# Fewer early key loads at the end of a projection stage, its weight conversions moved up, and its value copies moved to VectorE

## The chip, the cores and the metric

The kernel runs on one core of a Trainium2 chip. The metric is the device time in microseconds (us) of one execution; several executions are timed and their median counts. The engines are TensorE (PE, matrix products), VectorE (DVE), ScalarE (ACT), GpSimd (POOL) and SyncE (SP), which here issues every transfer on one queue of the core's 16 DMA engines.

## What is computed

A transformer layer over 4096 rows of 512 numbers: causal attention with 16 heads of 32, then a gated feed-forward net whose weights come as integers. In short:

```python
q, k, v = split(x @ Wqkv, 3)
q, k = layernorm(q) * q_ln_scale, layernorm(k) * k_ln_scale
attn = softmax(causal(q k^T / sqrt(32)))          # per head
x = layernorm(x + (attn @ v) @ out_W)
Wg, Wu, Wd = ((w - 128) * scale for w in (gate_w, up_w, down_w))
x = layernorm(x + (silu(x @ Wg^T) * (x @ Wu^T)) @ Wd^T)
```

## The kernel before

Three stages follow one another, each a block of its own with one program for each engine: `project` (to about 331 us), `attend` (to about 1540 us) and `finish`. What one stage hands to the next lies in DRAM or in buffers that all stages know (`keep`).

**The projection** walks over 8 chunks of 512 rows. A chunk has 12 units, one for each of its 4 row tiles and each of queries, keys and values (`m` = 0, 1, 2): PE multiplies a tile of rows with 512 columns of the weights, each number split into a high and a low part, so 12 products (L403) into one of four `acc` banks. For queries and keys DVE measures and normalises the rows (`measure`, `apply`); for values ACT copies the bank to `v_out` (`take_v`, L500 to 503) and SP stores it. The normalised rows of a chunk are then turned in 8 jobs (4 of queries, 4 of keys). For a job PE turns four 128x128 pieces (L425), ACT makes squares and the high half of the scaled result (`high`, L491 to 498), DVE the low half (`low`, L575), and SP stores both halves (L321). The halves lie in one of four part buffers, and ACT writes a buffer only once its former stores have landed (`parts_stored`).

The jobs of a chunk run beside the units of the next one. In the last chunk `plan` takes another order of the units (`final`): first the 8 units of queries and keys, beside which the jobs of the chunk before run, in units 1 to 7, and then the 4 units of values, 8 to 11, beside which the chunk's own 8 jobs run, two in each.

Beside all that the integer weights of the last stage are turned to float, 6 blocks of 256 KB a chunk: SP loads a block (L290), ACT turns it (`turn_float`, L510), DVE finds its largest number (`widest`, L601), SP stores it (L294). There are two buffers, so block e + 2 is loaded once block e is turned. Before the change block e is turned in unit 2e.

At the end of the projection DVE works out two flags from the largest norms and weights; the engines read them when the attention begins.

**Loads of the attention.** The attention takes its 4 groups of 4 heads one after the other, and in each group the 8 chunks of queries; chunk c meets c + 1 blocks of keys. A key load (`key_load`, L73 to 78) is three transfers of 256 KB, each to 32 partitions (high, low and high again), and for the first group one of 16 KB (`one_load`); a query load is three such transfers and one of 16 KB; a load of values is one of 256 KB. Each chunk's first score waits for its queries and its own key block. In the last chunk of the projection SP already issues loads for the first group, in `ahead(j)`, L333 to 349: with j = 0 keys 0, queries 0 and values 0, and with j = 1 and 2 keys 1 and 2. When the attention begins, SP issues, in this order, queries 1, [keys and] values 1, queries 2, [keys and] values 2, keys and values 3 to 7, stores of the context, and queries 3; keys below `AHEAD` are left out there.

Of the kernel before, what the change touches and what calls it, by code (L numbers as in the profile page):

```python
# [30 lines left out]
F32 = mybir.dt.float32  # L31
# [16 lines left out]
ST = CH // P  # L48
DC = D // P
# [7 lines left out]
BOUND = 60.0  # L57
WHOLE = 4096.0
ROWS = 3 * HD + 2
AHEAD = 3  # L60


def over_chunks(engine, body):
# [42 lines left out]
BLOCKS = 3 * IC // ST  # L106
# [21 lines left out]

def weight_load(sp, dr, keep, to, j):

    sp.dma_start(to.bitcast(F32), dr["wq"].rearrange("(b t) p d -> b p t d", t=ST)[j]).then_inc(keep["w_in"][j], 16)


def store_chunk(sp, dr, keep, g, ch):
# [26 lines left out]
def project(nc, io, dr, keep):  # L161


    ACCS = 4
    NU, NJ = 3 * ST, 2 * DC
# [4 lines left out]


    x_parts = {0: (0,), 1: (1, 2), 2: (3,)}

    def plan(before, after):

# [10 lines left out]
    with ExitStack() as c:  # L186
# [18 lines left out]
        v_out = sb("v_out", [P, 2, D])  # L205
# [25 lines left out]
        x_in = [sem(f"x_in{dc}") for dc in range(DC)]  # L231
        x_high = sem("x_high")
        x_low = sem("x_low")
        wqkv_in = [[sem(f"wqkv_in{dc}{m}") for m in range(3)] for dc in range(DC)]
        w_high_done = sem("w_high_done")
        w_low_done = sem("w_low_done")
        ident_ready = sem("ident_ready")
# [30 lines left out]
        @block.sync  # L268
        def _(sp):
            def load_x(n, dc):  # L270
                sp.dma_start(x_raw[:, dc, :], xs[dc][:, bass.ds(n * CH, CH)]).then_inc(x_in[dc], 16)

            for dc in range(DC):
                load_x(0, dc)
                for m in range(3):
                    cols = slice(m * D, (m + 1) * D)
                    sp.dma_start(w_raw[:, dc, cols], io["wqkv"][dc * P:(dc + 1) * P, cols]).then_inc(wqkv_in[dc][m], 16)
            sp.dma_start(scales[:, 0, :], io["q_scale"]).then_inc(scales_in, 16)
            sp.dma_start(scales[:, 1, :], io["k_scale"]).then_inc(scales_in, 16)
            sp.wait_ge(dconst, 1)  # L280
            for u in range(4):
                sp.dma_start(dr["shift"].rearrange("a h (p u s) -> u (a h p) s", u=4, p=4)[u], zeros[:]).then_inc(zero_stored, 16)
            sp.dma_start(dr["one_rows"].rearrange("a (h s) -> (a h) s", h=HG), one_fill[:]).then_inc(zero_stored, 16)
            sp.dma_start(ow_raw[:], io["out_w"].rearrange("(g r) e -> r g e", r=P)).then_inc(ow_in, 16)
            for s_, k in ((parts_stored, 32), (v_stored, 16), (wq_stored, 16)):
                for one in s_:
                    sp.sem_inc(one, k)

            def load_int(n, e):
                sp.dma_start(wq_int[:, e % 2, :], io["wq"][bass.ds(n * WT + e, 1)].rearrange("a p x -> (a p) x"))\  # L290
                  .then_inc(int_in[e % 2], 16)

            def store_float(n, e):
                sp.dma_start(dr["wq"][bass.ds(n * WT + e, 1)].rearrange("a p x -> (a p) x"), wq_f[:, e % 2, :])\  # L294
                  .then_inc(wq_stored[e % 2], 16)

            load_int(0, 0)
            load_int(0, 1)

            def body(n, c, par, before, after, half):  # L300
                for dc in range(DC if after else 0):

                    sp.wait_ge(x_low, DC * n + dc + 1)
                    sp.nop(nofuse=True)
                    load_x(n + 1, dc)
                for u, ((st, m), jobs) in enumerate(plan(before, after)):
                    if m == 2:
                        sp.wait_ge(v_taken, ST * n + st + 1)
                        sp.nop(nofuse=True)
                        sp.dma_start(dr["v"].rearrange("(t p) d -> t p d", p=P)[bass.ds(n * ST + st, 1)].rearrange("t p d -> (t p) d"),  # L310
                                     v_out[:, st % 2, :]).then_inc(v_stored[st % 2], 16)
                    for own, i in jobs:

                        o = n if own else c
                        sp.wait_ge(high_done, NJ * o + i + 1 + 2)
                        sp.nop(nofuse=True)
                        sp.wait_ge(low_done, NJ * o + i + 1 + 2)
                        sp.nop(nofuse=True)
                        g = i % DC
                        for part, to in ((part_hi, ("q_hi", "k_hi")), (part_lo, ("q_lo", "k_lo"))):  # L320
                            sp.dma_start(dr[to[i // DC]][g * P:(g + 1) * P, bass.ds(o * CH, CH)], part[:, i % 4, :].bitcast(F32))\  # L321
                               .then_inc(parts_stored[i % 4], 16)
                    if u % 2 == 0:
                        e = u // 2
                        sp.wait_ge(floated, WT * n + e + 1)
                        sp.nop(nofuse=True)
                        store_float(n, e)
                        if after or e + 2 < WT:
                            load_int(n, e + 2)
                    if not after and u in (1, 3, 5):  # L330
                        ahead(u // 2)

            def ahead(j):  # L333

                if j == 0:
                    sp.wait_ge(w_low_done, 3 * DC)
                    sp.nop(nofuse=True)
                    sp.wait_ge(zero_stored, 80)
                    sp.nop(nofuse=True)
                    for one in parts_stored:  # L340
                        sp.wait_ge(one, 32 + 64 * AHEAD)
                        sp.nop(nofuse=True)
                    for one in v_stored:
                        sp.wait_ge(one, 16 + 32)
                        sp.nop(nofuse=True)
                    sp.wait_ge(fin_pool, 1 + NG)
                    sp.nop(nofuse=True)
                key_load(sp, dr, keep, 0, j, keep["k_in"][j])
                one_load(sp, dr, keep, j, keep["k_in"][j])
                if j == 0:  # L350
                    query_load(sp, dr, keep, 0, 0, 0, keep["q_in"][0])
                    value_load(sp, dr, keep["first_values"][:], 0, 0, keep["v_in"][0])

            over_chunks(sp, body)
# [121 lines left out]
        def _(act):  # L476
# [35 lines left out]
            def body(n, c, par, before, after, half):  # L512
                for u, ((st, m), jobs) in enumerate(plan(before, after)):
                    if not before and u == 4:
                        act.wait_ge(ow_in, 16)
                        act.activation(ow_hi[:], ow_raw[:], ACT.Copy).then_inc(ow_high, 1)
                    if m == 1 and after and st in x_parts:

                        if before and st == 0:
                            act.wait_ge(acc_full, NU * n)  # L520
                        for dc in x_parts[st]:
                            high_x(n + 1, 1 - par, dc)
                    if m == 2:
                        take_v(n, u, st)
                    for own, i in jobs:
                        high(n if own else c, i)
                    if u % 2 == 0:
                        turn_float(n, u // 2)

            over_chunks(act, body)  # L530

# [1 line left out]
        def _(dve):  # L533
# [54 lines left out]
            def apply(n, par, u, st, i):  # L588
                dve.wait_ge(rstd_ready, 2 * ST * n + 2 * st + i + 1)
                dve.tensor_scalar(normed[:, par, i, st, :], acc[u % ACCS][:], mv[:, i, 0:1], rstd[:, i:i + 1],  # L590
                                  ALU.subtract, ALU.mult).then_inc(qk_normed, 1)

            def top(o, i):

                dve.wait_ge(norms_done, NJ * o + DC * (i + 1) + 2)
                dve.tensor_reduce(norm_max[:, i, bass.ds(o, 1)], norms[i][:], AX.X, ALU.max).then_inc(norms_read, 1)
# [6 lines left out]
            def body(n, c, par, before, after, half):  # L603
# [3 lines left out]
                for u, ((st, m), jobs) in enumerate(steps):  # L607
# [8 lines left out]
                    for t in tops:  # L616
                        if t[2] <= u:
                            top(*t[:2])
                    tops = [t for t in tops if t[2] > u]
                    for own, i in jobs:  # L620
                        low(n if own else c, i)
                        if i % DC == DC - 1:
                            tops.append((n if own else c, i // DC, u + 3))
                    if u % 2:
                        widest(n, u // 2)
                for t in tops:
                    top(*t[:2])

# [496 lines left out]
def finish(nc, io, dr, keep):  # L1125
# [7 lines left out]
    with ExitStack() as c:  # L1133
# [23 lines left out]
        slot = [[c.enter_context(nc.psum_tensor(f"slot{s}{b}", [P, CH], F32)) for b in range(2)] for s in range(2)]  # L1157
        y = [c.enter_context(nc.psum_tensor(f"y{st}", [P, D], F32)) for st in range(ST)]

        w_in, small_in = keep["w_in"], keep["small_in"]  # L1160
        ident_zero = sem("ident_zero")
        ident_ready = sem("ident_ready3")
        half_ready = sem("half_ready")
# [123 lines left out]
        def _(pe):  # L1287
# [50 lines left out]
            def program(v):  # L1338

                def gate_up(j, pos, n, par, i, first_chunk):  # L1340
# [3 lines left out]
                        pe.wait_ge(slot_free, t_end(n) + FREE)  # L1344
                    if first_chunk:
                        for j in range(3 * i // ST, (3 * i + 2) // ST + 1):
                            pe.wait_ge(w_in[j], 16)
                    for q in range(2):
                        w = tile(i, q)
                        for dc in range(DC):  # L1350
# [202 lines left out]
def build(nc, io):  # L1553
# [14 lines left out]
    with ExitStack() as c:  # L1568
# [9 lines left out]
            "q_in": [sem(f"q_in{b}") for b in range(3)],  # L1578
            "wq_stored": [sem(f"wq_stored{b}") for b in range(2)],
            "gate_scale": sb("gate_scale_sb", [P, IC], F32), "up_scale": sb("up_scale_sb", [P, IC], F32),  # L1580
            "small_in": sem("small_in"), "w_in": [sem(f"w_in{j}") for j in range(BLOCKS)],
            "ctx_in": [sem(f"ctx_in{h}") for h in range(HALF)], "x_res_in": [sem(f"x_res_in{h}") for h in range(HALF)],
            "inv_ready": sem("inv_ready"), "c_scaled": sem("c_scaled"), "c_high": sem("c_high"), "c_ready": sem("c_ready"),
            "ctx_taken": sem("ctx_taken"), "sums_taken": sem("sums_taken"),
# [53 lines left out]
```

## Time and profile before

| | us |
|---|---|
| runs of the kernel, median (lowest to highest) | 2370.82 (2368.36 to 2372.7) |
| the profiled execution | 2370.67 |
| its span, from first to last instruction | 2368.9 |

In that span PE is busy for 2308.9 us, DVE for 1775.2, ACT for 1291.7 and POOL for 245.3; the mean clock granted to TensorE is 0.988 of full speed. A row of a timeline gives the start and the duration in us, the engine, the line of the kernel, the operation, the tile that is written and those that are read, the shapes, how many instructions were merged, and in brackets how long the engine had been idle before and what ended that.

### The profile page before, as it was taken

Reading aid. Unit: us, or ns where it says so; the run is one execution under the profiler, and the core shown is the slowest. Engines: PE = TensorE matmul, PEld = TensorE weight load, DVE = VectorE, ACT = ScalarE, POOL = GpSimd, SP = SyncE. Lnnn points to the kernel's source line nnn. Section 1 sums busy time; section 2 is a strip of 40 time slices with the busy share of each in tenths; the row PEclk is TensorE's granted clock in tenths of the full one; section 3 lists DMA queues with packets and bytes.
Section 4 is the critical chain, followed back from the end, with each engine's and each line's share of the span. In section 5 each row is a group of like instructions: output and inputs, shape, how many; then the busy total and the mean of one; then the engine's idle time right before and its main releaser. Section 6 shows DMA issues by size and latency. Waiting matters only on the chain. (4 is left out here: it accounts for less than half of the span.)

```text
span 2368.9 us, 34364 instructions
## 1 busy us (share of the span) xinstructions
PE 2308.9 (97%) x12556; PEld 1424.3 (60%) x12578; DVE 1775.2 (75%) x1821; ACT 1291.7 (55%) x1631; POOL 245.3 (10%) x269
## 2 busy tenths in 40 slices
PE   8999979999999999999999999989999999999997
PEld 7888844444444444444444444378888888888885
DVE  7777748998889988899898998945556556465554
ACT  4444458888888888888888888711111111111111
POOL 2111112110021100211002110000000000000000
PEclk9999979999999999999999999989999999999998
DMA  7767785100821008210082101441111021110100
GB/s 252 254 238 252 231 255 106 33 23 6 179 56 33 24 6 170 60 33 24 6 165 64 33 24 41 147 151 36 36 36 54 22 69 36 37 54 18 36 19 18
DMA packets 126303, 197.50 MB, mean 83 GB/s; under 512 B 14489, under 2 KB 39577, under 8 KB 126113
## 3 DMA queue, kind: packets, MB, share of 16 engines
q1 hardware_dynamic: 126128, 195.25, 29.4%
q8 instruction: 101, 1.65, 0.3%
q14 instruction: 74, 0.60, 0.1%
HBM read 122.83 MB, written 72.37 MB: 82 GB/s over the span
## 5 line engine op out<-in xcount | busy, mean ns | idle before, releaser
L1041 ACT ACTIVATE probs<-score 128x1024 f32<-128x1024 f32 (+3 forms) x1152 | 1000.2, 970 | 176.1 <-PE score L953 174.6
L1104 DVE TENSOR_TENSOR total<-total,probs 128x2048 f32<-128x2048 f32 (+3 forms) x468 | 983.2, 2101 | 79.3 <-POOL probs L915 22.1
L953 PE MATMUL score<-queries,keys 98*128 98x512 f32 (+3 forms) x2304 | 641.7, 406 | 12.1 <-ACTq L1025 6.2
L953 PEld LDWEIGHTS score<-queries,keys 98*128 98x128 f32 x2304 | 380.9, 189 | 434.2 <-ACT probs L1041 350.3
L1416 ACT ACTIVATE hidden<-slot,gate_scale_sb 128x512 f32<-128x512 f32 x128 | 88.2, 689 | 633.8 <-PE slot L1352 633.8
L969 PE MATMUL ctx_acc<-probs,values 128*32 128x512 f32 (+3 forms) x3584 | 421.6, 561 | 0.0
L1478 DVE SCALAR_TENSOR_TENSOR hidden<-slot,up_scale_sb,hidden 128x512 f32<-128x512 f32 x128 | 96.0, 750 | 252.9 <-ACT hidden L1416 252.9
L915 POOL TENSOR_SCALAR_AFFINE_SELECT probs<-probs 128x512 f32<-128x512 f32 x128 | 167.3, 1308 | 1010.3 <-ACT probs L1041 1010.3
L1352 PE MATMUL slot<-xt_hi,w_front 128*128 128x512 f32 x608 | 238.5, 392 | 1.5 <-DVE xt_lo L1519 1.5
L1352 PE MATMUL slot<-xt_lo,w_front 128*128 128x512 f32 x608 | 238.1, 392 | 0.0
L969 PEld LDWEIGHTS ctx_acc<-probs,values 128*32 128x32 f32 x3584 | 85.5, 109 | 193.6 <-issue 148.6
L403 PE MATMUL acc<-w_hi,x_hi 128*128 128x512 f32 x384 | 164.2, 428 | 7.4 <-DVE w_lo L558 7.4
L1352 PE MATMUL slot<-xt_hi,w_back 128*128 128x512 f32 x416 | 163.4, 393 | 0.0
L1352 PE MATMUL slot<-xt_lo,w_back 128*128 128x512 f32 x416 | 162.1, 390 | 0.0
L403 PE MATMUL acc<-w_hi,x_lo 128*128 128x512 f32 x384 | 151.5, 394 | 0.0
L403 PE MATMUL acc<-w_lo,x_hi 128*128 128x512 f32 x384 | 151.0, 393 | 0.0
L969 PE MATMUL ctx_acc<-probs,first_values 128*32 128x512 f32 (+3 forms) x1024 | 132.8, 591 | 0.7 <-ACT ctx_out L1030 0.7
L1352 PEld LDWEIGHTS slot<-xt_hi,w_front 128*128 128x128 f32 x608 | 115.1, 189 | 26.2 <-DVE xt_lo L1519 1.7
L1352 PEld LDWEIGHTS slot<-xt_lo,w_front 128*128 128x128 f32 x608 | 115.0, 189 | 23.9
L1270 POOL TENSOR_TENSOR rstd<-veps,minus_half 128x1 f32<-128x1 f32 x64 | 36.2, 566 | 792.2 <-DVE veps L1442 792.2
L1363 PE MATMUL y<-w_front,h_hi 128*128 128x512 f32 x288 | 112.1, 389 | 0.0
L1363 PE MATMUL y<-w_front,h_lo 128*128 128x512 f32 x288 | 112.1, 389 | 0.0
(121 smaller groups left out, 2199.6 us busy)
## 6 DMA issues: line engine op xcount, KB each, us to landing
keys<-k_hi SPq DMA_DIRECT2D x64, 256.0 KB
queries<-q_hi SPq DMA_DIRECT2D x64, 256.0 KB
wq_int<-in_wq SPq DMA_DIRECT2D x48, 256.0 KB, 3.2
wq_float<-wq_f SPq DMA_DIRECT2D x48, 256.0 KB, 2.8
x_raw<-in_x_t SPq DMA_DIRECT2D x32, 256.0 KB, 3.7
v_rows<-v_out SPq DMA_DIRECT2D x32, 256.0 KB, 2.5
q_hi<-part_hi SPq DMA_DIRECT2D x32, 256.0 KB, 2.6
q_lo<-part_lo SPq DMA_DIRECT2D x32, 256.0 KB, 2.8
```

The source lines that it names most:

```text
L403: ins = pe.matmul(bank[:], x[:, par, dc, rows], w[:, dc, m * D:(m + 1) * D], start=dc == 0 and a == 0, stop=dc == DC - 1 and a == 2)
L915: pool.affine_select(out=view, in_=view, compare_op=ALU.is_ge, fill=0.0, base=0, pattern=[[0, HG], [1, P]], channel_multiplier=-1).then_in ...
L953: ins = pe.matmul(score[u % RING][:, i, cut(t):], keys[0:ROWS, kb // ST, h, kb % ST * P:(kb % ST + 1) * P], queries[0:ROWS, q_buffer[ch], ...
L969: ins = pe.matmul(ctx[h * HD:(h + 1) * HD, n0:], value(kb)[:, h * HD:(h + 1) * HD], probs[:, t % PB, h, n0:], start=t in first, stop=t in ...
L1041: act.activation(probs[:, t % PB, 2 * p:2 * p + 2, cut(t):], score[u % RING][:, :, cut(t):], ACT.Exp).then_inc(exped, 1)
L1104: dve.tensor_tensor(into, into, now, ALU.add).then_inc(added, 1)
L1270: pool.tensor_tensor(rstd[:, k, st:st + 1], veps[:, k, st:st + 1], minus_half[:], ALU.pow).then_inc(rooted[k], 1)
L1352: ins = pe.matmul(slot[pos % 2][q][:], v(w[:, dc * P:(dc + 1) * P]), v(x[:, par, dc, :]), start=dc == 0 and a == 0, stop=dc == DC - 1 and ...
L1363: ins = pe.matmul(y[st][:], v(x[:, st * P:(st + 1) * P]), v(tile(i, 2)), start=i == 0 and a == 0, stop=i == IC - 1 and a == 1)
L1416: act.activation(hidden[:, i % 2, :], slot[pos % 2][0][:], ACT.Silu, scale=gate_scale[:, i:i + 1]).then_inc(gated, 1)
L1478: dve.scalar_tensor_tensor(hid, slot[pos % 2][1][:], up_scale[:, i:i + 1], hid, ALU.mult, ALU.mult)\
```

## The change

- `AHEAD` is 1 in place of 3: of the loads for the attention only keys, queries and values 0 are issued in the projection, in unit 1 of the last chunk. Keys 1 and 2 are issued by SP in the attention, ahead of values 1 and 2.
- In the last chunk the six blocks of weights are turned in units 0, 1, 3, 4, 6 and 7 in place of 0, 2, 4, 6, 8 and 10. Their loads and stores on SP go with them, and DVE's reductions come one unit later each.
- In the last chunk DVE copies the values in place of ACT.
- The semaphores of the projection's weight loads are used again for the weight loads of the last stage, which now wait for 32 in place of 16.

```diff
-AHEAD = 3
+AHEAD = 1
...
-    sp.dma_start(to.bitcast(F32), dr["wq"].rearrange("(b t) p d -> b p t d", t=ST)[j]).then_inc(keep["w_in"][j], 16)
+    sp.dma_start(to.bitcast(F32), dr["wq"].rearrange("(b t) p d -> b p t d", t=ST)[j]).then_inc(keep["weights_in"][j], 16)
...
+    def float_units(after):
+
+        return [0, 2, 4, 6, 8, 10] if after else [0, 1, 3, 4, 6, 7]
...
-        wqkv_in = [[sem(f"wqkv_in{dc}{m}") for m in range(3)] for dc in range(DC)]
+        wqkv_in = [keep["weights_in"][3 * dc:3 * dc + 3] for dc in range(DC)]
...
-                    if u % 2 == 0:
-                        e = u // 2
+                    if u in float_units(after):
+                        e = float_units(after).index(u)
...
-                    if not after and u in (1, 3, 5):
-                        ahead(u // 2)
+                    if not after and u == 1:
+                        ahead(0)
...
-                    if m == 2:
+                    if m == 2 and after:
                         take_v(n, u, st)
...
-                    if u % 2 == 0:
-                        turn_float(n, u // 2)
+                    if u in float_units(after):
+                        turn_float(n, float_units(after).index(u))
...
+            def take_v(n, u, st):
+                dve.wait_ge(acc_full, NU * n + u + 1)
+                dve.wait_ge(v_stored[st % 2], 32 * n + 16 * (st // 2) + 16)
+                dve.tensor_copy(v_out[:, st % 2, :], acc[u % ACCS][:]).then_inc(v_taken, 1)
...
+                    if m == 2 and not after:
+                        take_v(n, u, st)
...
-                    if u % 2:
-                        widest(n, u // 2)
+                    if u - 1 in float_units(after):
+                        widest(n, float_units(after).index(u - 1))
...
-                            pe.wait_ge(w_in[j], 16)
+                            pe.wait_ge(w_in[j], 16 + 16)
```

## Rows read from the trace of the kernel before

**Rows 1.** Windows: start:end, length, busy us of each engine, granted clock, DMA share, GB/s
```profile
300.00:310.00 10.00, 7.02 (x37) 5.49 (x37) 4.30 (x7) 5.34 (x9) 0.54 (x1) 1.00 1.05 307
310.00:320.00 10.00, 6.75 (x30) 5.19 (x31) 3.41 (x5) 5.07 (x10) 0.00 (x0) 0.87 1.04 394
...
330.00:336.00 6.00, 0.08 (x1) 0.00 (x0) 0.80 (x4) 0.00 (x0) 0.00 (x0) 0.50 0.03 10
336.00:340.00 4.00, 3.71 (x10) 2.72 (x10) 0.00 (x0) 2.39 (x3) 0.32 (x1) 0.50 0.52 140
340.00:384.00 44.00, 44.00 (x278) 19.17 (x277) 34.72 (x22) 34.95 (x47) 15.74 (x12) 0.91 1.09 202
...
400.00:500.00 100.00, 99.82 (x632) 42.70 (x624) 93.14 (x46) 85.73 (x98) 11.39 (x9) 1.00 0.13 33
```

**Rows 2.** Timeline of ACT in the last chunk of the projection
```profile
296.59 0.69 ACT L497 ACTIVATE squares<-turn,mix_root 128x512 bf16<-128x512 f32 x1 [2.57 <-DMA q_lo<-part_lo]
297.18 0.68 ACT L498 ACTIVATE part_hi<-turn,scales 128x512 fp32r<-128x512 f32 x1
297.78 0.63 ACT L510 ACTIVATE wq_f<-wq_int 128x512 f32<-128x512 int32 x1
...
315.46 0.69 ACT L497 ACTIVATE squares<-turn,mix_root 128x512 bf16<-128x512 f32 x1 [1.25 <-issue]
...
322.76 0.60 ACT L503 ACTIVATE v_out<-acc 128x512 f32<-128x512 f32 x1 [1.74 <-PE acc L403]
```

**Rows 3.** Timeline of PE, the turns of the last chunk's own parts
```profile
303.48 0.63 PE L425 MATMUL turn<-ident,normed_qk 128*128 128x128 f32 x4 [1.25 <-DVE normed_qk L590]
...
307.59 0.60 PE L425 MATMUL turn<-ident,normed_qk 128*128 128x128 f32 x4
309.92 0.63 PE L425 MATMUL turn<-ident,normed_qk 128*128 128x128 f32 x4 [1.72 <-ACT part_hi L498]
...
317.61 1.09 PE L425 MATMUL turn<-ident,normed_qk 128*128 128x128 f32 x4 [1.67 <-ACT part_hi L498]
...
322.57 0.60 PE L425 MATMUL turn<-ident,normed_qk 128*128 128x128 f32 x4
```

**Rows 4.** Timeline of SP: the first issue of keys 1 and of keys 2
```profile
291.18 0.45 SPq L76 DMA_DIRECT2D keys<-k_hi  x1
...
296.40 0.60 SPq L76 DMA_DIRECT2D keys<-k_hi  x1
```

**Rows 5.** Timeline of PE in the attention: first scores, chunk 1's, chunk 3's
```profile
336.29 5.89 PE L953 MATMUL score<-queries,keys 98*128 98x512 f32 x16 [6.21 <-ACTq L1025]
...
343.98 2.08 PE L953 MATMUL score<-queries,keys 98*128 98x512 f32 x4
...
385.73 1.66 PE L953 MATMUL score<-queries,keys 98*128 98x512 f32 x6 [0.88 <-DMA queries<-shift]
```

**Rows 6.** Integer blocks, 289 to 303 us: durations min/median/max in ns, starts, landing
```profile
L290 SPq DMA_DIRECT2D wq_int<-in_wq x3: 552/670/929, 289.5 to 302.2; - x3
...
DMA to landing us min/median/max: 8.2/11.9/12.1
```

**Rows 7.** Timeline of DVE: last normalised rows, last reduction of a block, flags
```profile
302.54 0.80 DVE L590 TENSOR_SCALAR normed_qk<-acc,mv,rstd 128x512 f32<-128x512 f32 x1
...
326.62 0.67 DVE L601 TENSOR_REDUCE whole<-wq_f 128x1 f32<-128x512 f32 x1
...
330.75 0.16 DVE L641 CAST flags<-flag_f 1x2 int32<-1x2 f32 x1
```

**Rows 8.** Loads of values 2 and of values 7: issue and landing, columns as rows 6
```profile
L99 SPq DMA_DIRECT2D values<-v_rows x1: 400/400/400, 341.4 to 341.4; - x1
...
DMA to landing us min/median/max: 8.4/8.4/8.4
...
L99 SPq DMA_DIRECT2D values<-v_rows x1: 393/393/393, 366.4 to 366.4; - x1
...
DMA to landing us min/median/max: 15.1/15.1/15.1
```

More of the change, by code:

```diff
@@ L1158, in finish @@
         y = [c.enter_context(nc.psum_tensor(f"y{st}", [P, D], F32)) for st in range(ST)]
-        w_in, small_in = keep["w_in"], keep["small_in"]
+        w_in, small_in = keep["weights_in"], keep["small_in"]
         ident_zero = sem("ident_zero")
@@ L1580, in build @@
             "gate_scale": sb("gate_scale_sb", [P, IC], F32), "up_scale": sb("up_scale_sb", [P, IC], F32),
-            "small_in": sem("small_in"), "w_in": [sem(f"w_in{j}") for j in range(BLOCKS)],
+            "small_in": sem("small_in"), "weights_in": [sem(f"weights_in{j}") for j in range(BLOCKS)],
             "ctx_in": [sem(f"ctx_in{h}") for h in range(HALF)], "x_res_in": [sem(f"x_res_in{h}") for h in range(HALF)],
```

## The prediction

> **What bounds the kernel now.** I read the windows first, then the timelines of ScalarE (ACT), TensorE (PE), VectorE (DVE) and SyncE (SP) over the end of the projection, then the landings of single transfers, then PE at the start of the attention. In the attention PE is busy 99.8% of the time [rows 1], so whatever delays PE there is paid in full, and two places matter: the last chunk of the projection and the first 60 us behind it. In the last chunk the DMA engines are saturated: their share is 1.05 and 1.04 in 300 to 320 us [rows 1], while PE is busy 7.02 and 6.75 of each 10 us. The ACT rows show why. A part buffer (four of them) can be written again only when its stores have landed, and the squares wait for exactly that, 2.57 us for the low half of queries at 296.59 [rows 2]; where the row says "issue" (at 315.46) it is the same wait in the code. PE waits behind ACT: its turns stand idle 1.25, 1.72 and 1.67 us [rows 3], and at 317.61 four turns take 1.09 us in place of 0.63: after these gaps the granted clock fell to 1.2 GHz (mean 0.87 in 310 to 320 [rows 1]). The cause of the queue is in the SP rows: two further blocks of keys are fetched in the middle of it [rows 4]. Behind the projection the DMA engines idle, work at a share of 0.52 in 336 to 340, and then at 1.09 for the 44 us to 384 [rows 1]. That stretch ends on PE's path too: the first scores of chunk 3 wait 0.88 us for the last piece of its queries [rows 5].
>
> **Part 1: keys 1 and 2 leave the projection.** Two key loads are six transfers of 256 KB plus two of 16 KB, 1.61 MB. What it gives: without them the queue is gone by the time the last chunk's own eight parts run. Then PE goes from the first turn (303.48) to the seventh (322.57) [rows 3] without the waits. One pair of turns and one unit take 307.59 - 303.48 = 4.11 us, with no wait between them; there are three such periods, 12.3 us in place of 19.1 us. That is 6.8 us.
>
> **Part 2: floats two units earlier.** No instruction is added; six turnings, stores and integer loads keep their count. But ACT works in order, and turning block 4 now stands in unit 6, ahead of the squares of unit 7. Its integers are loaded in unit 3, at about 292 (where SP issued keys 1 at 291.18 [rows 4], and 0.9 us for the store and load that now stand ahead of chunk 0's loads). Integer loads took 8.2 to 12.1 us to land in this queue [rows 6]; the 8.2 belongs to the one that was not behind keys 1, so it lands at 300.2. From there: the turning to 300.9 (0.63), squares and high half to 302.2 (0.59 + 0.68) [rows 2], the low half to 302.9 (taken like the reduction, 0.7), the reduction to 303.5, the last normalised rows to 304.3 (0.80) [rows 7]. PE's first turn came right behind those rows (302.54 + 0.80, PE 303.48), so it moves to 304.4: a loss of 0.9 us. If the load takes 12.1 us the loss is 4.8 us; if it isn't late at all, zero.
>
> **Part 3: values by DVE.** Four copies leave ACT (0.60 us each [rows 2]) and go to DVE, where they cost about as much. DVE has room: it is busy 4.30 of 10 us and 3.41 of 10 us there [rows 1]. On the path the last copy holds ACT to 323.36 while the seventh turn has ended at 323.17: 0.2 us. The last reduction of a float block (326.62, 0.67 us, of which 0.6 before the next) leaves the end of DVE's chain to the flags: 0.6 us. If DVE's cover were gone the copies would cost 4 x 0.6 = 2.4 us.
>
> **The sum for the projection** is 6.8 - 0.9 + 0.2 + 0.6 = 6.7 us, between 2.8 (late integers) and 7.6. The flags, written at 330.75 [rows 7], come at about 324, and SP, PE and ACT start the attention as much earlier; the gap of 5 us behind the flags, with a DMA share of 0.03 [rows 1], stays. Shared semaphores and waits on 32 cost nothing: the weight loads of the last stage are counted from what the projection left, with no new producer.
>
> **Part 4: what comes back.** SP issues keys 1 now between queries 1 and values 1, keys 2 behind queries 2, and everything up to the queries of chunk 3 is queued behind them. Chunk 1's first score ran at 343.98 without a wait [rows 5]. It will wait for keys 1: at most 1.61 / 2 MB at 202 GB/s, 4.0 us, at least nothing; I take 2.5 us. This is not paid twice, since PE later waits again. At chunk 3 the queue decides: PE is there at 384.85 (385.73 - 0.88), its queries land at 385.73, and 1.61 MB more stand ahead of them. At the 202 GB/s of 340 to 384 [rows 1] this is 8.0 us. By landings it is more: values 2, issued at 341.4, landed 8.4 us later; values 7, issued at 366.4, 15.1 us later [rows 8]; 31.7 us for five pairs of keys and values, 6.3 us a pair, less 1.3 us for the 256 KB of values at 202 GB/s, 5.0 us a key load, 10.1 us for two. The lower end is the 394 GB/s of the stores in 310 to 320 [rows 1], 4.1 us. I take 9.0, between the two values of the stretch itself.
>
> In 340 to 384 the engines are as full (1.09) as in 310 to 320 (1.04) and move half as much. The Trainium skill has a rule for this (SBUF — State Buffer, Door 1: The DMA port swizzle): a transfer to 32 partitions reaches 8 of the 16 ports, and partitions 0 to 63 no more, so it gets half the bandwidth, 218 GB/s at most. Each piece of a key or query load goes to 32 partitions; by that figure the two loads would cost an estimated 7.4 us in the attention, and the trace's 202 GB/s agrees. The rule speaks against the change: loads of this kind are moved from beside stores, which use all partitions, to a stretch of loads of their own kind.
>
> **The clock.** PE stands still at chunk 3 from about 387.4 to 394.7 (in times of the kernel before), far longer than the gaps after which the clock fell at 317. It would restart at 1.2 GHz. At the start of the attention PE resumed at 336.29 and the clock came back at about 347.9 (0.91 mean over 44 us: 7.9 us of it at half), 11.6 us later [rows 1, 5]; six full scores took 1.66 us at full clock, four 2.08 us at half [rows 5], so PE loses about 0.45 us a microsecond: between 0 and 5.2 us. I take half, 2.6 us.
>
> **Sum.** -6.7 + 9.0 + 2.6 = +4.9 us. The profiled execution took 2370.67 us (span 2368.9 and 1.8 around it), the median of the runs is 2370.82: both are the same to 0.01%. 2370.67 + 4.9 = 2375.6 us.
>
> **Rivals.** (a) The stall at chunk 3 leaves the clock alone: +2.3 us, 2373.0. For it: gaps up to 1.72 us left it alone. Against: this gap is four times that. (b) Not slower: the two loads run in the attention at the stores' rate, 4.1 us, because SP issues keys 1 in 336 to 340, where the share is 0.52. Then -6.7 + 4.1 = -2.6, 2368.1. It decides at 6.7 us for the two, 240 GB/s; for over 0.2% faster they would have to cost under 2 us. Against: keys 1 are issued behind queries 1, and from 340 the engines are full. (c) The integers of block 4 are late as in the kernel before (12.1 us): the projection gives 2.8 in place of 6.7, in all +8.8, 2379.5. For it: the queue of chunk 0's loads stands ahead of them still. Against: keys 1 no longer do.
>
> **How the numbers follow.** A measurement of this kernel tells 0.2% (4.7 us) from no change, so "same" is 2366.1 to 2375.5. The forecast has 0.50, with its own range 2372 to 2380; (a) 0.18, (b) 0.14, (c) 0.18. Slower by over 0.2%: half of the forecast, nearly all of (c), little of (a): 0.45. Faster: under half of (b) and a remainder, 0.08. Same: 0.47. The range is 2367.5 (most of (b)) to 2381.
>
> **What would show it.** Squares in units 8 to 11 without waits for landings; the flags near 324; a wait of PE for keys 1 of about 2.5 us, then one of 5 to 8 us for the queries of chunk 3, and a granted clock of 0.5 behind it; windows near 100% after. The forecast is wrong if the wait at chunk 3 is under 3 us, or if the flags come later than 327.

## The result, and the profile after

| | before | after |
|---|---|---|
| median, us (20 runs each, side by side) | 2371.38 | 2375.56 |
| lowest to highest, us | 2368.36 to 2376.03 | 2371.91 to 2378.26 |
| ratio to before, 95% interval | 1 | 1.0017 (1.0012 to 1.0023) |
| profiled execution, us (its span) | 2370.67 (2368.9) | 2375.79 (2374.0) |

The changed kernel is slower by 4.2 us of the medians; that is little, but the interval leaves 1 out. 2375.6 us was predicted.

First the windows, with the columns of [rows 1]:

```profile
300.00:310.00 10.00, 7.43 (x30) 5.75 (x30) 6.44 (x12) 4.84 (x8) 0.55 (x1) 0.83 0.99 376
310.00:320.00 10.00, 9.59 (x54) 7.86 (x54) 5.58 (x8) 5.74 (x10) 0.00 (x0) 1.00 0.72 273
...
340.00:384.00 44.00, 40.55 (x264) 17.41 (x264) 33.07 (x20) 33.05 (x42) 10.30 (x8) 0.93 1.09 204
384.00:396.00 12.00, 7.21 (x28) 3.58 (x32) 5.04 (x3) 5.23 (x6) 0.64 (x1) 0.72 0.28 65
400.00:500.00 100.00, 99.82 (x639) 42.56 (x642) 92.95 (x47) 85.11 (x101) 14.65 (x10) 1.00 0.13 33
```

The window from 384 us before the change, which [rows 1] leaves out:

```profile
384.00:396.00 12.00, 10.85 (x67) 4.53 (x63) 7.90 (x4) 9.59 (x13) 1.27 (x2) 1.00 0.07 21
```

In 310 to 320 us PE is busy 9.59 of 10 us (6.75 before) while the DMA share has gone from 1.04 to 0.72: the queue in this part of the projection is gone. But in 340 to 384 PE, which was busy all 44 us before, loses 3.45 us with the DMA engines as full as they were (1.09), and in 384 to 396 it works 7.21 of 12 us, where it was 10.85, at a mean granted clock of 0.72, where it was 1.00. From 400 us on the windows agree.

The timelines give the places. PE and DVE at the end of the projection, to be held against [rows 3] and [rows 7] (the second and third row are the first products of unit 9):

```profile
304.37 0.63 PE L429 MATMUL turn<-ident,normed_qk 128*128 128x128 f32 x4 [2.57 <-DVE normed_qk L594]
...
305.51 0.90 PE L407 MATMUL acc<-w_hi,x_hi 128*128 128x512 f32 x1
306.21 0.63 PE L407 MATMUL acc<-w_lo,x_hi 128*128 128x512 f32 x1
...
318.18 0.60 PE L429 MATMUL turn<-ident,normed_qk 128*128 128x128 f32 x4
...
325.78 0.16 DVE L652 CAST flags<-flag_f 1x2 int32<-1x2 f32 x1
```

First to seventh turn take 13.81 us instead of 19.09, and the flags come 4.97 us sooner, at 325.78. ACT shows what delays the first turn (compare [rows 2]):

```profile
297.97 0.69 ACT L501 ACTIVATE squares<-turn,mix_root 128x512 bf16<-128x512 f32 x1 [4.36 <-DMA q_lo<-part_lo]
...
300.34 0.63 ACT L514 ACTIVATE wq_f<-wq_int 128x512 f32<-128x512 int32 x1 [1.10 <-DMA wq_int<-in_wq]
300.87 0.67 ACT L501 ACTIVATE squares<-turn,mix_root 128x512 bf16<-128x512 f32 x1
...
302.94 0.63 ACT L514 ACTIVATE wq_f<-wq_int 128x512 f32<-128x512 int32 x1 [0.81 <-DMA wq_int<-in_wq]
```

The integers of two blocks arrive after ACT has come to them (1.10 and 0.81 us), and behind these no squares name a landing any more. Ahead of them the squares still wait for one, 4.36 us and to 297.97, where it was 2.57 us and to 296.59. Then SP's first issue of the attention and PE's scores, against [rows 5]:

```profile
330.96 2.53 SPq L89 DMA_DIRECT2D queries<-q_hi  x2
```
```profile
331.25 5.89 PE L964 MATMUL score<-queries,keys 98*128 98x512 f32 x16 [6.14 <-ACTq L1036]
...
343.03 2.05 PE L964 MATMUL score<-queries,keys 98*128 98x512 f32 x4 [4.03 <-issue]
...
388.79 3.78 PE L964 MATMUL score<-queries,keys 98*128 98x512 f32 x8 [5.21 <-DMA queries<-shift]
```

The attention starts 5.04 us sooner, chunk 1 only 0.95 us sooner, because PE now waits 4.03 us there; chunk 3 starts 3.06 us later than before, after a wait of 5.21 us, and its scores run at half clock (eight take 3.78 us where six took 1.66). Matched product by product with the kernel before, PE's delay grows from 3.06 us there to 5.05 us at 400 us: the half clock accounts for the rest of the 5.1 us of span.

### The profile page after: what moved, and what is told of

It reads as the page before. It is cut to its first block and busy times, and to the rows that moved or that the text cites. A ratio compares the mean times of both kernels' runs of the same rounds, so it can differ in the third digit from the quotient of the medians.

```text
span 2374.0 us, 34368 instructions
## 1 busy us (share of the span) xinstructions
PE 2311.5 (97%) x12556; PEld 1425.5 (60%) x12578; DVE 1778.2 (75%) x1825; ACT 1289.6 (54%) x1627; POOL 246.8 (10%) x269
```

## Experiments

Each ratio is to the kernel before, run beside it on the same chip; three kernels were run once and stand outside the table. "The distance" is the time from SP's first issue of queries 1 to the first score of chunk 3, wherever PE waited for that: it is what the queue of the attention costs, with the start of the attention taken out. It is 49.85 us before (335.88 to 385.73) and 57.83 us after (330.96 to 388.79).

Flags, distances and waits are those of one profiled execution each. With the code of the projection unchanged the flags came at 328.69 to 331.41 us in four kernels (before, before with queries 3 early, narrow, wide), and at 323.34 and 326.89 in the two with keys 1 in unit 9. So two kernels' flags that lie less than about 3.5 us apart are not told from each other by them.

| kernel | ratio (95%) | flags at | distance | wait at chunk 3 |
|---|---|---|---|---|
| before | 1 | 330.75 | 49.85 | 0.88 |
| changed | 1.0017 (1.0012 to 1.0023) | 325.78 | 57.83 | 5.21 |
| loads alone | 1.0007 (0.9997 to 1.0016) | 323.64 | 56.84 | 0.78 |
| units alone | 1.0002 (0.9992 to 1.0011) | 332.45 | 49.12 | 1.28 |
| changed, queries 3 early | 0.9994 (0.9985 to 1.0004) | 324.24 | | none |
| before, queries 3 early | 0.9990 (0.9981 to 0.9999) | 331.41 | | none |
| changed, keys behind the stores | 1.0004 (0.9995 to 1.0014) | 326.56 | 49.65 | 2.11 |
| keys 1 in unit 9 | 0.9995 (0.9986 to 1.0004) | 323.34 | 52.44 | 3.75 |
| keys 1 in unit 9, queries 3 early | 0.9976 (0.9967 to 0.9985) | 326.89 | | none |
| keys 1 and 2 in units 9 and 10, queries 3 early | 0.9976 (0.9967 to 0.9985) | 323.94 | | none |
| the same as keys 1 in unit 9, queries 3 early, with the units of the change | 0.9966 (0.9955 to 0.9977) | 324.99 | | none |

### Which half does what

**The loads alone.** Only keys 0 are loaded in the projection; the floats and the copies of values stay as before.

```diff
-AHEAD = 3
+AHEAD = 1
...
-                    if not after and u in (1, 3, 5):
-                        ahead(u // 2)
+                    if not after and u == 1:
+                        ahead(0)
```

> Only keys 1 and 2 leave the projection; the floats keep units 0, 2, 4, 6, 8, 10 and ACT keeps the copies of the values. Theory (the queue of transfers holds the last chunk's turns; the two key loads come back ahead of the queries of chunk 3): the flags come 4 to 6 us earlier than in the kernel before, the attention loses 8 us at chunk 3 and 2 us of clock behind it: 4 to 6 us slower than before, about as the changed kernel, and the moved floats and copies are worth less than 2 us either way. Rival (it is the moved floats and copies that shorten the projection): the flags come less than 2 us earlier and the time is 8 us or more above the kernel before.

Measured: 2373.28 us against 2371.01, 2.3 us of the medians, smaller than expected and not told from nothing by the interval. PE and DVE:

```profile
340.71 2.05 PE L953 MATMUL score<-queries,keys 98*128 98x512 f32 x4 [3.39 <-issue]
...
386.06 1.66 PE L953 MATMUL score<-queries,keys 98*128 98x512 f32 x6 [0.78 <-DMA queries<-shift]
```
```profile
323.64 0.16 DVE L641 CAST flags<-flag_f 1x2 int32<-1x2 f32 x1
```

The flags come 7.1 us sooner: the projection's gain comes from the loads. That it is more than with the whole change (4.97 us) lies inside the scatter named above; 1.57 of the 2.14 us is the clock, which fell at the first turn in the changed kernel's profiled execution and not here (first to seventh turn 13.81 and 12.24 us). The queries of chunk 3 land 56.84 us after the first issue, 7.0 us more than before. That PE waited only 0.78 us for them isn't a better queue: PE was late itself. Its clock stayed at half until 354.1 us, after the wait for chunk 1; matched with the kernel before, PE was 6.73 us early at its first scores and 0.45 us late at 359 us, so that this wait of 3.39 us cost 7.2.

**The units alone.** Floats in units 0, 1, 3, 4, 6, 7 and values by DVE, keys 1 and 2 in the projection as before.

```diff
-                    if u % 2 == 0:
+                    if u in float_units(after):
...
-                    if m == 2:
+                    if m == 2 and after:
                         take_v(n, u, st)
...
```

> Only the floats and the copies of the values are moved; keys 1 and 2 stay in units 3 and 5 of the last chunk. Theory: the attention is as in the kernel before (wait of 0.9 us at chunk 3, no fall of the clock there); the projection gains little, 0 to 2.5 us, because the queue stays: 0 to 2.5 us faster than before. Rival (floats and copies are the gain): the flags come 4 us or more earlier, 4 to 5 us faster than before.

Measured: 2371.74 us against 2371.01, not told from no change. The flags came at 332.45, later than in all four executions of the old projection, not earlier. ACT, then PE at chunk 3, then the window behind it:

```profile
302.71 0.63 ACT L514 ACTIVATE wq_f<-wq_int 128x512 f32<-128x512 int32 x1 [1.99 <-DMA wq_int<-in_wq]
...
309.62 0.63 ACT L514 ACTIVATE wq_f<-wq_int 128x512 f32<-128x512 int32 x1 [5.13 <-DMA wq_int<-in_wq]
```
```profile
386.92 1.66 PE L964 MATMUL score<-queries,keys 98*128 98x512 f32 x6 [1.28 <-DMA queries<-shift]
```
```profile
384.00:396.00 12.00, 10.45 (x50) 3.86 (x42) 6.96 (x4) 6.70 (x8) 0.64 (x1) 0.72 0.14 38
```

This is the lateness of rival (c) seen by itself: with the keys still in the queue the integers are late by 1.99 and 5.13 us, and the first turn comes at 306.74. Only the tail gains: from the seventh turn to the flags 7.60 us, where it was 8.18, which is the last reduction taken off.

### What the queue of the attention costs

**Narrow and wide.** In both, the kernel before gets six more transfers of 256 KB in the attention, all between queries 1 and values 1 (the changed kernel has its second key load behind queries 2). They go to the places of keys 6 and 7, so SP also waits for them before it issues keys 6. In the first they are shaped as key loads are, 32 partitions each; in the second the same rows go to 128 partitions.

```diff
                     load("q", 1)
+                    for k in range(2):
+                        for r, src in enumerate(("k_hi", "k_lo", "k_hi")):
+                            sp.dma_start(keys[r * HD:(r + 1) * HD, NCH - 1 - k, :, :]...)   # narrow
+                            sp.dma_start(keys[:, NCH - 1 - k, r, :]...)                     # wide
                     load("kv", 1)
...
+                        if j == NCH - 2:
+                            sp.wait_ge(spare_in, 96)
...
```

> The kernel before, with six further transfers of 256 KB in the attention, between queries 1 and values 1, of the shape of key loads (32 partitions, four pieces of 2 KB each) into key blocks that are loaded only later. Nothing reads them; the result is the same. Theory: 1.57 MB at the 202 GB/s of that stretch, 7.8 us more until the queries of chunk 3 land: the wait there grows from 0.9 to 8 to 9 us, the clock falls, and the time is 9 to 12 us above the kernel before. Rival (the queue has room): the wait grows by less than 4 us.

> As the run with six further transfers of the shape of key loads, from the same rows of DRAM, but each into 128 partitions with one piece of 2 KB. Theory (the target's 32 partitions set the rate, as the rule of the Trainium skill on ports has it): 1.57 MB at up to the 394 GB/s of the stores, 4 us or less until the queries of chunk 3 land: a wait of 3 to 5 us there. Rival (the source rows, 16 KB apart, or the number of pieces set the rate): the same wait of 8 to 9 us as with the narrow transfers.

Measured: one execution each, 2379.73 and 2374.88 us against a median of 2369.62. SP's first issue and PE at chunk 3, narrow, then wide:

```profile
336.10 1.99 SPq L89 DMA_DIRECT2D queries<-q_hi  x2
```
```profile
391.78 3.78 PE L961 MATMUL score<-queries,keys 98*128 98x512 f32 x8 [7.11 <-DMA queries<-shift]
```
```profile
334.29 1.92 SPq L89 DMA_DIRECT2D queries<-q_hi  x2
```
```profile
387.83 3.78 PE L960 MATMUL score<-queries,keys 98*128 98x512 f32 x8 [5.03 <-DMA queries<-shift]
```

The distance is 55.68 us narrow and 53.54 us wide: 5.8 and 3.7 us more than before, for the same 1.57 MB from the same rows. By those, the narrow ones moved at 270 GB/s and the wide ones at 425 (1.57 MB over the added time). So the number of partitions that a transfer fills bears on its rate here, as the prediction supposed; it is one execution each, and the 2.1 us between them stand against differences of 0.7 and 1.0 us in the distance between kernels whose queue is alike (49.85 and 49.12, 57.83 and 56.84). The Trainium skill's rule (SBUF — State Buffer, Door 1: The DMA port swizzle) gives 32 partitions half of the bandwidth, 218 GB/s at most; the two runs agree with its direction, but the ratio is 1.6 and not 2, and 270 GB/s is above its figure, with other transfers running in between.

**The rows of ones.** The real key loads cost 7.0 to 8.0 us and the narrow copies 5.8. The key loads also bring two small transfers of 16 KB, which fill two rows. This kernel is the changed one with these two issued in the projection.

```diff
+                    for later in (1, 2):
+                        one_load(sp, dr, keep, later, keep["k_in"][later])
...
-                        if before is None:
+                        if before is None and j > 2:
                             one_load(sp, dr, keep, j, k_in[j])
```

> The changed kernel, but the two 16 KB transfers of ones that belong to keys 1 and 2 are issued in the projection, behind values 0. The six transfers of the same bytes as in the run with narrow loads then stand alone in the queue. In the changed kernel queries 1 to chunk 3's first score took 57.8 us, in the kernel before 49.9, with the six narrow transfers 55.7. Theory (each transfer of ones is two pieces of 8 KB, 0.4 to 0.9 us each on one of the 16 engines, and the last engine decides when the queries have landed): 55.5 to 56.5 us, a wait of 3 to 4 us at chunk 3. Rival (the difference of 2.1 us between the two runs is scatter, or comes from the place of keys 2): 57.5 us or more, a wait as before of 5 us.

Measured: one execution, 2377.59 us against 2371.23. PE at chunk 3:

```profile
390.48 3.78 PE L966 MATMUL score<-queries,keys 98*128 98x512 f32 x8 [5.10 <-DMA queries<-shift]
```

The distance is 56.65 us, 1.2 us less than in the changed kernel and 0.2 us less than with the loads alone, whose queue in the attention is the changed kernel's. It lies between both expectations, and the wait itself is unchanged. Inconclusive: where the difference between copies and real key loads comes from stays open.

### Taking the wait at chunk 3 away

**Changed, queries 3 early.** The queries of chunk 3 are issued behind keys and values 3, ahead of those of chunks 4 to 7 and not behind them.

```diff
                         load("kv", j)
+                        if j == 3:
+                            load("q", 3)
...
-                    if before is not None or ch > 2:
+                    if before is not None or ch > 3:
                         load("q", ch)
```

> The changed kernel with one line moved in the attention's first group: the queries of chunk 3 are issued right behind keys and values 3 in place of behind keys and values 7. Theory (the loss is a place in the queue, not the load on it): the wait of 5.2 us at chunk 3 and the half clock behind it go, the wait of 4.0 us for keys 1 stays; 6 to 8 us faster than the changed kernel, so 1 to 3 us faster than the kernel before. Rival (the two loads cost their time wherever the queries stand, because the stretch is full): PE waits as long at chunk 3 or 4, and less than 2 us come back.

Measured: 2369.94 us against 2371.01. The changed kernel stands 4.2 us above before, this one 1.1 us below, with an interval that includes no change. The wait at chunk 3 and the fall of the clock behind it are gone, so both were due to the queue ahead of these queries.

**Before, queries 3 early.** The same edit in the kernel before.

> The kernel before with only the queries of chunk 3 moved behind keys and values 3. Theory: the wait of 0.9 us at chunk 3 goes, the rest stays: 0.5 to 2 us faster than the kernel before. Rival (queries 3 ahead of keys 4 to 7 make another chunk wait): 0 or slower.

Measured: 2368.63 us against 2371.23, 2.6 us less, with no wait at chunk 3 and a granted clock of 1.00 behind it; the interval ends just short of no change (0.9981 to 0.9999). It gives more than the 0.88 us of [rows 5]. The profiled execution of before does not show why; in the kernel with the units alone a wait of 1.28 us at this place brought the half clock, so other executions of before may well pay it. That is argued, not shown.

### Where keys 1 and 2 can be loaded instead

**Behind the stores.** The changed kernel, with keys 1 and 2 issued in the projection after its last stores.

```diff
-AHEAD = 1
+AHEAD = 3
...
+                if not after:
+                    ahead(1)
+                    ahead(2)
```

> The changed kernel, but keys 1 and 2 are issued in the projection again, behind the last stores of its last chunk, where the DMA engines idle for some 6 us while the flags are made and read. Theory: projection as in the changed kernel (flags about 5 us earlier than before), attention as in the kernel before (no wait for keys 1, about 1 us at chunk 3): 3.5 to 5.5 us faster than the kernel before. Rival (SP's eight issues of 3.5 us, or loads that are not done when the attention begins, delay queries 1): the attention begins 2 to 4 us later and nothing is left of the gain.

Measured: 2371.95 us against 2371.01, not told from no change: the rival came true. The flags come at 326.56, but the first score runs 10.6 us behind them where it was 5.5. DVE's first instruction of the attention (it follows the barrier between the stages), PE's first score, and two windows:

```profile
329.29 0.09 DVE L1071 MEMSET ones<- 128x32 f32 x1 [2.58 <-PEq L190]
```
```profile
337.12 5.89 PE L967 MATMUL score<-queries,keys 98*128 98x512 f32 x16 [11.24 <-ACTq L1039]
```
```profile
326.00:330.00 4.00, 0.00 (x0) 0.00 (x0) 0.73 (x4) 0.00 (x0) 0.00 (x0) 0.50 0.88 205
330.00:334.00 4.00, 0.00 (x0) 0.00 (x0) 0.00 (x0) 0.00 (x0) 0.00 (x0) 0.50 0.95 198
```

In the changed kernel the same DVE instruction waits 1.27 us, and the score follows it by 4.05 us instead of 7.83. The first 1.3 us are SP's: it issues the keys until 327.8, so it comes later to the barrier. Of the other 3.8 us most lies in PE's branch into the attention, of which the trace keeps a record outside these views: it lasts 6.77 us here, 3.47 us before and 3.43 us in the changed kernel, and 3.41 to 4.03 us in all kernels but this one and the one with keys 1 and 2 in units 9 and 10. While it lasts, the DMA engines are full here (0.88 and 0.95), and all but idle before (0.03 [rows 1]). The Trainium skill (Runtime: NRT & Kernel Launch, Instruction fetch mechanics) says that a branch to a page not yet held makes a DMA fetch that page before execution goes on; the profile's DMA view agrees, with packets of instruction queues in this stretch. Their records in the trace show where the time goes: the 16 KB packet of one of these queues starts 1.04 us behind the branch in the changed kernel and 4.04 us behind it here, and PE's branch ends 2.4 and 2.7 us after that.

**Keys 1 in unit 9.** Keys 1 are loaded in the last third of the chunk, when the queue has shrunk, keys 2 in the attention; floats and copies as before. The first kernel also issues queries 3 behind keys and values 3, the second does not.

```diff
-AHEAD = 3
+AHEAD = 2
...
-                    if not after and u in (1, 3, 5):
-                        ahead(u // 2)
+                    if not after and u in (1, 9):
+                        ahead(u // 8)
```

With queries 3 moved:

> The kernel before with three moves: keys 1 are issued in unit 9 of the last chunk, behind that unit's stores, in place of unit 3; keys 2 in the attention, behind queries 2; and the queries of chunk 3 behind keys and values 3. Floats and copies of values stay as before. Theory: the projection is as short as in the run where only the key loads left it (flags some 7 us earlier), since the only stores behind keys 1 are those of the last four parts, for which no one waits there; no wait for keys 1 at chunk 1, none at chunk 3, the clock back some 12 us after the first scores as before: 6 to 8 us faster than the kernel before. Rival (any key load in the last units holds the turns again, or is still in the queue when the engines branch into the attention): less than 3 us faster.

Without:

> As the fastest run (keys 1 in unit 9, keys 2 in the attention), but the queries of chunk 3 stay behind keys and values 7. Theory: one key load more ahead of them, some 4 us in that queue: a wait of 4 to 6 us at chunk 3 and the half clock behind it, 5 to 8 us slower than the fastest run, so 0 to 2 us from the kernel before. Rival (the place of the queries is worth only the 0.9 us that the kernel before waited): within 2 us of the fastest run.

Measured: 2363.56 us against 2369.62 with the move, which beats both kernels; 2370.17 against 2371.23 without, not told from no change. In the second the distance is 52.44 us, 2.6 us for the one key load that is left in the queue (two cost 7.0 to 8.0, more than twice that). PE comes to chunk 3 early and waits, and the clock falls again:

```profile
381.61 3.49 PE L953 MATMUL score<-queries,keys 98*128 98x512 f32 x8 [3.75 <-DMA queries<-shift]
```

In the first the wait at chunk 1 is gone as well. What that wait costs is read from a comparison with the changed kernel with queries 3 early, which differs at this place only in it. PE at chunk 1 and at the second group of scores of chunk 3, and a window, of that kernel:

```profile
330.25 5.89 PE L966 MATMUL score<-queries,keys 98*128 98x512 f32 x16 [6.67 <-issue]
...
341.39 2.04 PE L966 MATMUL score<-queries,keys 98*128 98x512 f32 x4 [3.38 <-issue]
...
387.10 0.73 PE L966 MATMUL score<-queries,keys 98*128 98x512 f32 x2 [0.20 <-ACT probs L1054]
```
```profile
344.00:354.00 10.00, 10.00 (x45) 4.22 (x37) 4.02 (x2) 6.53 (x8) 1.27 (x2) 0.50 1.09 197
```

The same of the kernel with keys 1 in unit 9 and queries 3 moved:

```profile
332.64 5.89 PE L955 MATMUL score<-queries,keys 98*128 98x512 f32 x16 [6.42 <-ACTq L1027]
...
381.76 0.73 PE L955 MATMUL score<-queries,keys 98*128 98x512 f32 x2 [0.20 <-ACT probs L1043]
```
```profile
344.00:354.00 10.00, 10.00 (x74) 4.35 (x72) 6.80 (x4) 8.63 (x12) 4.01 (x3) 1.00 1.11 198
```

From the first score to that group it is 56.85 us with the wait and 49.12 us without, for the same number of products: the 3.38 us cost 7.73. (In the last kernel below, which differs from the first of these two only in the place of keys 1, it is 48.87 us.) The rest is the clock, which had fallen at the end of the projection and with the wait came back at 354.9 us only, in the other kernel at 343.3. The rows do not name the transfer that PE waits for at chunk 1 ("issue"): queries 1 are issued just ahead of keys 1. That the wait is gone once keys 1 are loaded earlier shows that their load is its cause, whichever of the two PE waits for.

**Both keys there.** Keys 2 in unit 10 too, so `AHEAD` stays at 3; queries 3 are moved as before. The edit is against the kernel before.

```diff
-                    if not after and u in (1, 3, 5):
-                        ahead(u // 2)
+                    if not after and u in (1, 9, 10):
+                        ahead((1, 9, 10).index(u))
```

> As the run with keys 1 in unit 9, but keys 2 in unit 10 as well. Theory: 1.6 MB in a queue that the stores fill to some 70% from 310 us on does not empty by the time the flags are written (some 8 us of work in 12 us with 30% free): the loads are still running while the engines branch into the attention, and the branch takes longer, as in the run with both loads behind the last stores (6.8 in place of 3.5 us). So 1 to 4 us slower than with keys 1 alone. Rival (the queue empties in time): the same time as with keys 1 alone, within 1 us.

Measured: 2364.94 us against 2369.62, no better than keys 1 alone. The flags come at 323.94, but the first score runs 8.2 us behind them, where it is 5.75 with keys 1 alone. PE's branch takes 5.10 us of that (3.74 with keys 1 alone), with the DMA engines still busy with keys 2:

```profile
332.12 5.89 PE L955 MATMUL score<-queries,keys 98*128 98x512 f32 x16 [8.86 <-ACTq L1027]
```

**With the units of the change.** Keys 1 in unit 9, queries 3 moved, and floats and copies as the change has them.

> The fastest run with the floats in units 0, 1, 3, 4, 6, 7 and the copies of values on DVE, as in the changed kernel. Theory: in a queue without keys 1 and 2 these parts cost the wait for block 4's integers ahead of the squares of unit 7 (about 1 us at the first turn) and give back 0.6 us at the flags: within 1.5 us of the fastest run, rather slower. Rival (they are worth something once the queue is short): 1.5 us or more faster than the fastest run.

Measured: 2363.91 us against 2371.23. Against the same kernel without them the two ratios' intervals overlap (0.9955 to 0.9977, 0.9967 to 0.9985): what the earlier floats and the copies by DVE are worth can't be told from nothing here.

## Why the prediction was right

| step | predicted | profiled |
|---|---|---|
| integers of block 4 turned at | 300.2 | 300.34 |
| first turn at | 304.4 | 304.37 |
| first to seventh turn, us | 12.3 | 13.81 |
| seventh turn to the flags, change in us | -0.8 | -0.58 |
| projection, us | -6.7 | -4.97 |
| wait at chunk 1, us | 2.5, at most 4.0 | 4.03 |
| queue up to chunk 3, us | +9.0 (4.1 to 10.1) | +7.98 |
| wait at chunk 3, us | 5 to 8 | 5.21 |
| clock behind it, us | +2.6 (0 to 5.2) | +2.0 |
| sum, us | +4.9 | +5.1 |

The mechanism was as forecast in its main steps, and both halves have a run that shows it: the loads alone give the projection its gain and the attention its queue, and with queries 3 moved the loss at chunk 3 and its clock are gone. The closeness of the sum is partly luck: the errors cancel, the profiled times are of one execution, and the twenty executions of the changed kernel lie between 2371.91 and 2378.26 us.

**Part 1** (6.8 us for three periods) was 1.5 us too high in the profiled execution, for a reason the sum did not hold: the clock fell at the first turn, after an idle time of 2.57 us, and the products of unit 9 took 0.63 us each. In the changed kernel with queries 3 early, whose projection is the same code, it did not fall (after 2.39 us): first to seventh turn 12.21 us, the flags at 324.24, where "about 324" was said. The loads alone (12.24 us) agree with it. So the period was sized rightly, and whether the clock falls there varies between executions. The 19.1 us that it was taken from varies as well: the same code took 19.00, 16.93 and 16.42 us in three other kernels (before with queries 3 early, narrow, wide), so the 6.8 us are the gain over one execution, and by the others it would be less. I had used the fall at 317 in the kernel before as a reading, and not asked whether the later first turn brings one of its own.

**Part 2** was right in its mechanism: the integers stand in the queue of chunk 0's loads, and the 8.2 us of [rows 6] was the row to take. In all five kernels with the new units and without keys 1 and 2 in that queue ACT waits 1.10 to 1.18 us for block 4. That the first turn came within 0.1 us of the forecast is luck: in these five it came between 304.37 and 306.81 us, because the landing that the squares ahead of block 4 wait for moved from 297.97 to 300.34, a wait that the sum did not hold. The kernel with the units alone shows the late case, as in rival (c).

**Part 3** was right in the tail. That ACT is freed of the copies shows nowhere as time.

**Part 4** took 9.0 us for two key loads, between 8.0 (the stretch's 202 GB/s) and 10.1 (landings of pairs); 8.0 and, in the loads alone, 7.0 were measured. The rate of the stretch was the better row: in the 31.7 us between the two landings of [rows 8] the engines moved 198 GB/s, 6.3 MB, and the five pairs are 5.3 of them, so the landings charged the pairs with other transfers too. The rival that the loads run at the stores' rate (4.1 us) is refuted by these, and the wide copies show what it would have taken: to 128 partitions nearly the same bytes cost 3.7 us.

**The wait at chunk 1** came out at its upper bound, and "not paid twice" held: PE's arrival at chunk 3 is late by it, and the wait there is shorter by as much. What the step missed is that such a wait can also keep the clock down. In the changed kernel's profiled execution it did not: PE's delay over it, matched with the kernel before, is 3.8 us for the wait of 4.03. With the loads alone and with queries 3 moved it is 7.2 us for 3.4. In the changed kernel a longer delay here would make the wait at chunk 3 shorter, as the loads alone show with 0.78 us, so the sum did not need it; with queries 3 moved it is the largest loss that is left.

**The clock** behind chunk 3 cost 2.0 us for 2.6; half clock lasted from 387.5 to 394.4 us. Rival (a), that it stays at full, did not occur in any run with a wait above 1.2 us there.

## What to carry to other kernels

Loads taken out of a full stretch have a price where they go: ask which transfer ends last behind them there, and move that one along, since the place of one chunk's queries in the order was worth about 5 us here, with keys 1 in the projection or behind it. Price a transfer by rows of its own shape, as the same bytes cost 5.8 us to 32 partitions and 3.7 us to 128, and price a wait of PE with the clock behind it. A gap with idle DMA engines between two stages need not be free room: the branch into the next stage fetches its instructions through it.

## What the runs showed of the hardware that was not expected

- The branch of PE into the next stage lasted 3.41 to 4.03 us in twelve kernels, with a DMA share of 0.04 to 0.29 while it lasted; 5.10 us with keys 2 still landing (0.59), and 6.77 us with both loads running (0.69). The 16 KB packet of an instruction queue began 1.03 to 1.68, 2.59 and 4.04 us behind the branch, and the first score came 5.4 to 6.1, 8.2 and 10.6 us behind the flags.
- In the attention the clock fell after single waits of 1.28, 2.11, 3.75, 5.0 to 5.2 and 7.11 us, and did not after 0.78 and 0.88. At the first turn of the last chunk it fell after 2.03 us in one kernel (wide); after 3.07 us it fell in one (keys behind the stores) and did not in another (keys 1 in unit 9, queries 3 and the units).
- It came back late: 15.3 us after the first score in the changed kernel, 24.6 us with the loads alone, 11.8 us before, at 1.2 GHz (a granted clock of 0.50) all that time. Why a wait of 4.03 us delayed it less than one of 3.39 is open.
